# Three-layer attention and MLP kernel on one core: the first group gets a program of its own, one product for the gates, a token-major down product, and x normalised by ScalarE

## The reference

```
x  = x + proj(attention(q from ada_ln(x), k, v from ada_ln(ctx)))          # CROSS0
s  = silu(cond) @ W_mod + b_mod      -> shift_a scale_a gate_a shift_m scale_m gate_m
x  = x + gate_a * proj(self_attention(ln(x) * (1 + scale_a) + shift_a))    # SELF1
x  = x + proj(attention(q from ln(x), k, v from ln(ctx)))                  # CROSS1
h  = gelu((ln(x) * (1 + scale_m) + shift_m) @ W_mlp1 + b_mlp1)
x  = x + gate_m * (h @ W_mlp2 + b_mlp2)                                    # MLP
```

## Time and profile before

| | |
|---|---|
| median of 3 runs | 320.36 us (318.62 to 321.75) |
| the profiled execution's own time | 321.06 us |
| its span | 319.3 us |
| busy: PE, DVE, ACT, POOL | 273.6, 237.2, 199.4, 129.5 us |
| first scores of unit 0 start (PE L440) | 31.50 us |
| unit 0's attention is transposed (PE L493) | 57.41 us |
| unit 47's attention is transposed (PE L493) | 290.60 us |
| last DVE instruction ends | 316.5 us |

### The profile page before, as it was taken

How to read it: one execution, slowest core, us unless ns; L and a number is a source line. 1 busy time by engine, 2 the same in 40 slices (tenths; PEclk the granted TensorE clock), 3 DMA queues, 4 the chain that set the end, 5 groups by cost and what they waited for, 6 DMA issues and landing times.

```text
span 319.3 us, 9897 instructions
## 1 busy us (share of the span) xinstructions
PE 273.6 (86%) x3731; PEld 172.9 (54%) x3731; DVE 237.2 (74%) x503; ACT 199.4 (62%) x344; POOL 129.5 (41%) x257
## 2 busy tenths in 40 slices
PE   0555669799999899999999999999999899989983
PEld 0422345566656566566666666666666555544441
DVE  6854884977979879789798897988979796311422
ACT  2234236558686776677666666677676768799560
POOL 8553832723525235253472654636435131200100
PEclk9985756969999999999999999999999999999999
DMA  6953331321323414133141331312414100000112
GB/s 194 285 162 109 99 104 42 101 66 30 107 71 89 117 53 118 52 89 103 54 114 41 102 106 52 101 55 78 129 54 114 43 4 4 3 3 1 33 33 66
DMA packets 31902, 25.36 MB, mean 79 GB/s; under 512 B 4552, under 2 KB 31600, under 8 KB 31856
## 3 DMA queue, kind: packets, MB, share of 16 engines
q1 hardware_dynamic: 30240, 23.49, 26.3%
q10 hardware_dynamic: 1616, 1.25, 1.4%
HBM read 4.41 MB, written 1.05 MB: 17 GB/s over the span
## 4 chain that ended last, share of the span: by engine, by line
PE 55%; DVE 26%; issue 8%; ACT 8%; POOL 1%; ACTq 1%; DVEq 0%; POOLq 0%
DVE neg_max L838 13%; PE all_ps L477 11%; PE all_ps L415 9%; PE score_ps L440 5%; PE keyed_ps L463 5%; PE all_ps L508 4%; PE all_ps L517 4%; PE all_ps L405 4%; PE all_ps L500 3%; PE all_ps L488 3%; DVE x_stats L805 3%; ACT parts L636 3%; PE all_ps L398 2%; DVE r_sum L853 2%; DVE normed L819 2%
## 5 line engine op out<-in xcount | busy, mean ns | idle before, releaser
L838 DVE TENSOR_REDUCE neg_max<-score_ps 128x8 f32<-128x1024 f32 x96 | 116.9, 1218 | 9.3 <-PE score_ps L440 8.6
L656 ACT ACTIVATE probs<-keyed_ps 128x1024 f32<-128x1024 f32 x96 | 98.4, 1025 | 18.4 <-PE keyed_ps L463 18.2
L477 PE MATMUL all_ps<-probs,values 128*32 128x128 f32 x1536 | 62.1, 282 | 2.1 <-ACT probs L656 2.1
L477 PEld LDWEIGHTS all_ps<-probs,values 128*32 128x32 f32 x1536 | 37.0, 110 | 21.2 <-issue 9.5
L440 PE MATMUL score_ps<-stack_k,stack_q 62*128 62x128 bf16 x768 | 40.0, 227 | 9.6 <-DVE neg_max L838 9.6
L664 ACT ACTIVATE summed<-all_ps 128x256 f32<-128x256 f32 x48 | 18.4, 383 | 38.0 <-PE all_ps L477 38.0
L440 PEld LDWEIGHTS score_ps<-stack_k,stack_q 62*128 62x128 bf16 x768 | 22.7, 97 | 32.0 <-DVE neg_max L838 20.9
L463 PE MATMUL keyed_ps<-stack_q,stack_k 64*128 64x128 bf16 x768 | 38.6, 221 | 0.7 <-ACT probs L656 0.7
L989 POOL CAST max_parts<-neg_max 128x16 bf16<-128x16 f32 x48 | 10.1, 210 | 65.1 <-DVE neg_max L838 65.0
L621 ACT ACTIVATE normed_t<-all_ps,mod 128x128 f32<-128x128 f32 x48 | 18.0, 460 | 28.9 <-PE all_ps L405 18.8
L982 POOL TENSOR_TENSOR rstd<-var_eps,minus_half 128x4 f32<-128x4 f32 x24 | 25.4, 1059 | 18.0 <-DVE var_eps L807 18.0
(11 more groups left out here) (97 smaller groups left out, 395.6 us busy)
## 6 DMA issues: line engine op xcount, KB each, us to landing
stack_q<-parts SPq DMA_DIRECT2D x72, 128.0 KB, 2.4
stack_k<-parts SPq DMA_DIRECT2D x72, 128.0 KB, 2.4
stack_q<-max_rows SPq DMA_DIRECT2D x96, 4.0 KB
xs<-in_x_dram SPq DMA_DIRECT2D x4, 256.0 KB, 7.0
cs<-in_ctx_dram SPq DMA_DIRECT2D x4, 256.0 KB, 6.4
out_dram<-xs SPq DMA_DIRECT2D x4, 256.0 KB, 2.3
w<-in_L_xcond_W_mlp_dram SPq DMA_DIRECT2D x2, 256.0 KB, 4.2
wmod<-in_L_xcond_W_mod_dram ACTq DMA_DIRECT2D x1, 384.0 KB, 4.3
```

Source lines behind the costliest of these rows:

```text
L477: mm = pe.matmul(ps[QUAD * a:QUAD * (a + 1), c * T:(c + 1) * T], values[:, u // PER % STACKS, u % PER * PAIRS + CP * c + a, 2 * e:2 * e + ...
L656: act.activation(probs[:, n % 3, :], keyed_ps[:, :, :].rearrange("t e n -> t (e n)"), ACT.Exp, scale=float(D) ** -0.5).then_inc(probs_read ...
L838: dve.tensor_reduce(neg_max[:, u % 2, :, CP * c:CP * (c + 1)], score_ps[:, :, :].rearrange("t e (a k) -> t e a k", k=T), AX.X, ALU.max, ne ...
```

## The change

- **Head.** The first group is taken out of the tick loop: each engine has a straight program for `setup` and the front of group 0, and the loop starts at tick -6 rather than -10. `cond` is transposed before silu. DVE modulates the first context tile and splits the first k; ACT issues the first group's six k moves. The fills of the rings stand in other places. The late modulations move from tick 0 to tick 2.
- **Gates.** One product of 16 rows by 256 columns in tick 1; its rows go to DRAM and sixteen DMAs, one a tick, spread them over 128 partitions. `c_rep` is no longer filled, and the eight gate ticks are gone.
- **Normalising x.** POOL also computes minus the mean and the offset; ACT writes `normed` for x. The context stays on DVE.
- **Order.** `project_v` takes its bank before `project_qk(g, 0)`; ACT's second half of `modulate` for x comes behind the exponential; SP's moves are re-ordered.
- **MLP.** The down product has tokens as its rows, 8 steps of 2 sequences, 8 products of 128 columns each. The transposes back and ACT's bias step are gone; POOL adds gate times bias to x beforehand. Stores are halved in size.

```diff
+        gate_d = nc.dram_tensor("gate_d", [B, 2 * H], F32, kind="Internal").ap()
...
-        FIRST = -10
+        FIRST = -6
         LAST = 57
-        GATES_AT = (16, 19, 20, 23, 24, 27, 28, 31)
-        UP_AT = (43, 43, 44, 44, 45, 46, 46, 46, 47, 47, 48, 48, 52, 52, 52, 52)
-        DOWN_AT = (48, 48, 49, 49, 49, 49, 50, 50, 50, 50, 50, 50, 53, 53, 53, 53)
-        TURN_AT = (49, 50, 52, 55)
-        GELU_AT = (48, 49, 50)
+        UP_AT = (41, 43, 44, 45, 46, 46, 46, 48, 48, 48, 49, 49, 52, 53, 53, 53)
+        DOWN_AT = (49, 49, 50, 50, 51, 51, 53, 56)
+        GELU_AT = (48, 50, 51)
+        ADD_AT = (49, 50, 50, 51, 51, 51, 52, 53)
+        ACT_NORMS = (0,)
...
+            def put_gates():
+                sp.wait_ge(gate_rows_ready, 1)
+                sp.dma_start(gate_d, gate_rows[:, :, :].rearrange("b a h -> b (a h)")).then_inc(gate_put, 16)
+
+            def spread_gate(b):
+                if b == 0:
+                    sp.wait_ge(gate_put, 16)
+                sp.dma_start(gate[:, b, :, :].rearrange("t a h -> t (a h)"),
+                             gate_d[b:b + 1, :].broadcast_to([128, 2 * H])).then_inc(gate_landed, 16)
...
+            def gates():
                 w = wmod[:, :].rearrange("k (a n) -> k a n", n=H)[:, 2:6:3, :]
+                pe.matmul(take("gate")[0:B, 0:2 * H], c_col[:, :], w, start=True, stop=True).then_inc(gate_ps, 1)
...
+                pe.wait_ge(hidden_ready, MLP * (q + 1))
+                ps = take("down", 2 * q + c)
+                for j in range(2):
+                    for i in range(MLP):
+                        mm = pe.matmul(ps[:, j * H:(j + 1) * H], hidden_of(q, i)[:, (2 * c + j) * T:(2 * c + j + 1) * T],
+                                       w2[:, i, :], start=(i == 0), stop=(i == MLP - 1))
+                mm.then_inc(mlp_ps, 1)
 
             setup()
+            transpose_normed(0, 0)
+            transpose_normed(0, 1)
+            project_qk(0, 0)
+            project_qk(0, 1)
+            project_v(0)
...
+            def normalise_act(g, n):
...
+                for j in range(PER):
+                    ins = act.activation(normed[:, n, j, :], src[:, b0 + j, :], ACT.Identity,
+                                         bias=offset[:, n, j:j + 1], scale=rstd[:, n, j:j + 1])
+                ins.then_inc(normed_ready[n], 1)
...
+            modulate(0, 0, True)
+            modulate(0, 0, False)
+            first_part(0, 0)
+            first_part(0, 1)
+            act.wait_ge(hi_ready, 2)
+            act.wait_ge(stack_ones, 1)
+            for t in (0, 3, 5):
+                act.dma_start(stack_k[t:128:LANE, 0, :, :], parts[:, 0, 1, 0, :]).then_inc(k_landed[0], 16)
+            copy_values(0)
+            act.wait_ge(k0_split, 1)
+            for t in (1, 4):
+                act.dma_start(stack_k[t:128:LANE, 0, :, :], parts[:, 0, 1, 1, :]).then_inc(k_landed[0], 16)
+            act.wait_ge(k0_split, 2)
+            act.dma_start(stack_k[2:128:LANE, 0, :, :], parts[:, 0, 1, 2, :]).then_inc(k_landed[0], 16)
...
+            def add_mlp_bias(q):
...
+                pool.tensor_tensor(gate_b[:, :, :], gate[:, PER * q:PER * (q + 1), 1, :],
+                                   b_mlp[:, :].unsqueeze(1).broadcast_to([128, PER, H]), ALU.mult).then_inc(gate_b_ready, 1)
...
+                pool.wait_ge(normed_ready[0], GROUPS + q + 1)
+                pool.tensor_tensor(xs[:, PER * q:PER * (q + 1), :], xs[:, PER * q:PER * (q + 1), :],
+                                   gate_b[:, :, :], ALU.add).then_inc(x_biased, 1)
```

More of the change, by code:

```diff
@@ L45 @@
 RINGS = (("all", 4),)
-RING_KINDS = (("attn", "max", "turn", "proj", "out", "cond", "mod", "bias", "late", "norm", "q", "k", "v", "gate", "mlp", "up", "down"),)
+RING_KINDS = (("attn", "max", "turn", "proj", "out", "cond", "mod", "bias", "late", "norm", "q", "k", "v", "gate", "up", "down"),)
 R_Q, R_K, R_V = (0, 3, 6), (1, 4, 7), (2, 5, 8)
@@ L234, in at_tick @@
             uses += [("norm", g, 1)] * (g is not None)
+            g = attention(front(tick, -7))
+            uses += [("v", g)] * (g is not None)
             g = attention(front(tick, -8))
             uses += [("q", g)] * (g is not None)
-            g = attention(front(tick, -7))
-            uses += [("v", g)] * (g is not None)
-            uses += [("gate", i) for i in range(B // 2) if GATES_AT[i] == tick]
             uses += [("turn", tick - 1)] * unit(tick - 1)
@@ L556, in _ @@
                     keyed_scores(tick, 1)
+                g = attention(front(tick, -7))
+                if g is not None:
+                    project_v(g)
                 g = attention(front(tick, -8))
@@ L571, in _ @@
                     attend(tick, 0)
-                for n in range(MLP * B // PER):
+                if tick == 1:
+                    gates()
+                for n in range(B // 2):
                     if DOWN_AT[n] == tick:
-                        mlp_down(n // MLP, n % MLP)
-                if tick in TURN_AT:
-                    turn_mlp(TURN_AT.index(tick))
+                        mlp_down(n // 2, n % 2)
         @block.scalar
@@ L721, in _ @@
                     modulate(g, 0, False)
-                if unit(tick):
-                    exponentials(tick, 1)
-                g = front(tick, -8, 1)
+                for n in range(MLP * B // PER):
+                    if UP_AT[n] == tick:
+                        leave_hidden(n)
+                g = attention(front(tick, -7))
                 if g is not None:
-                    modulate(g, 1, False)
+                    copy_values(g)
                 g = attention(front(tick, -8))
@@ new lines, in modulate_context, with split_first_k @@
+            def modulate_context():
+                dve.wait_ge(normed_ps[1], 1)
+                dve.wait_ge(mod_ready, 2)
+                for j in range(PER):
+                    ins = dve.tensor_scalar(normed_t[:, 1, j, :], bank("norm", 0, 1)[:, j * T:(j + 1) * T],
+                                            mod[:, M_KV_SCALE, j:j + 1], mod[:, M_KV_SHIFT, j:j + 1], ALU.mult, ALU.add)
+                ins.then_inc(normed_t_ready[1], 1)
+            def split_first_k():
+                dve.wait_ge(rest_ready, 2)
+                dve.tensor_copy(parts[:, 0, 1, 1, :], rest[:, 1, :]).then_inc(k0_split, 1)
+                dve.wait_ge(k0_split, 1)
+                dve.tensor_tensor(parts[:, 0, 1, 2, :], rest[:, 1, :], parts[:, 0, 1, 1, :], ALU.subtract).then_inc(k0_split, 1)
```

345 lines of the change are left out of this document (186 added, 159 removed).

## The result

The changed kernel takes 305.26 us (median of 4 runs, 304.43 to 307.22) where the kernel before, run beside it, takes 320.97; the ratio is 0.955 with an interval of 0.951 to 0.959. The profiled execution took 304.43 us, with a span of 302.6. The forecast was 298.5, the range 290 to 307. So the size came out inside the range, at the value of the first rival (305), and 6.8 us above the forecast. One execution of a later kernel (joined, with the fillers) took 310.93 us at a granted clock of 0.85 for nearly its whole length, where the three others took 297.60 to 299.34, and is left out of its figures.

A forecast was written before the change was run, and what follows sets the result against it. PE was taken to set the loop's pace, with DVE close behind. Gates -7.7, loop -3.0, head -6, start-up -3 and tail -2.4 summed to -22.1 from 321.06, so 299.0; the forecast was 298.5 us, range 290 to 307.

The forecast's parts named there:

- the first rival: Loop gives nothing beyond the gates, ACT's load and later k moves taking the order's gain: about 305 us, chance 0.15.
- Gates, -7.7: In the loop's eight gate ticks, sixteen 256-column products go, all on PE's path: 7.7 us less.
- The loop's order, -3.0: In the loop, v-product and exponential waits go, DVE is relieved, ACT's normalising costs: -3.0 us, between -6 and +2.
- the +2.1: In the loop, ACT's normalising of x delays what PE needs by 0.2 us a group over eleven groups: +2.1 us.
- The gain of -1 from DVE's relief: In the loop, taking x's normalising off DVE relieves 1 us of PE's 4.2 us wait for row maxima.
- The head, -6: Before the first scores: they come at about 25.5 instead of 31.50 us; -6 us, between -3 and -8.
- the prediction's own sign of being wrong: In the head: the prediction is wrong if the first scores come after 29 us.
- The start-up, -3: At the loop's start, moved work and no c_rep fill give back half-clock time: -3 us, between 0 and -5.
- The tail, -2.4: At the MLP end, bias, transposes and waits shrink while down products grow dearer: -2.4 us, between +1 and -4.
- The second: Loop and start: all 8.3 us of waits go and the clock stays up, 3 us more: about 290, chance 0.10.
- the fourth: Head and tail move nothing that counts: half clock eats the earlier start, token-major products cost 0.29 each; 309, chance 0.06.

The follow-up runs named there:

- joined, with the fillers: Changed kernel plus MLP's x normalised by DVE, two POOL fills kept clear, ACT's group-1 normalising and a ring fill earlier, nine unread PE products: 297.64 us, ratio 0.932.
- the run with the gates alone: Kernel before with only the gates changed: one product at tick 1, rows spread through DRAM by 16 DMAs, no c_rep; 313.35 us, ratio 0.980.
- the run with the fills kept clear: Changed kernel with POOL's first two fills of values delayed until DVE normalised the first context and split the first k; 304.93 us, ratio 0.950.

## Why the prediction was right or wrong

The traced executions are 16.7 us apart, where -22.1 was forecast. Gates and order together gave the loop 6.5 of 10.7, the head 2.5 of 6 to the first scores, the start-up more than its 3, the tail 2.2 of 2.4. That the sum fell inside the range is in part luck: two of the five terms failed, a third gave more than forecast, and the tail's came out as the difference of two amounts that were not in it. Two sums are also off as written: 0.2 us over eleven groups is 2.2 and not 2.1, and the start-up's parts add up to -2.7, rounded to -3.

**Gates, -7.7: size near, working wrong.** Their run gave 6.9. But "all of it is on the path" failed: of 7.7 us of products the loop gave back 5.2, since half of the gate ticks also had a wait that overlapped them. What made up for it stood in another term: the `c_rep` fill that went with the gates gave 2.6 us at the start-up. So I had that money in two places.

**The loop's order, -3.0: failed, it gave 1.3.** Three steps. First, "The v product now takes its bank ahead of q, so 2.3 us of waits should go": they stayed, 2.3 us. Four banks back from v stands k, both before and after; q is taken in another tick, so the exchange of the two changes nothing there. Counting the ring back by its length in the order of uses would have shown it. Second, the waits for exponentials did go as predicted; the modulation in one piece brings back 2.7 us. Third, ACT's four instructions take 1.65 us, not 1.4, and they cost the loop half of the +2.1: 0.13 us in one tick of four, 1.1 together, through `summed`, as the run with x on DVE shows. The gain of -1 from DVE's relief did not come as a wait gone: between units 4 and 36 PE waits 3.9 us for the maxima, 4.0 in the run with the gates alone. But in the new order DVE could not have kept the work for nothing, it would cost 1.2 us.

**The head, -6: too large, by wrong placing.** The first scores moved 2.5 us, to 29.03, just past the prediction's own sign of being wrong. The stall was real, with 3.20 us for four instructions and 2.41 for a cast, but the step "Last come the context tiles of group 1, on DVE, beside POOL's fills" named the wrong tiles. The first fill stands right behind the inverse root of the context of group 0 and meets its normalising, ahead of every product; the second meets the cast of k. Here the rule of the Trainium skill (SBUF — State Buffer, Who interferes with whom) bears on it: the trace agrees that a fill holds DVE up, 0.45 us against 2.41 for the same cast, and what I missed was only when each fill runs. The same thing spoils a reading: the 1.61 us of the earlier trace rows at 4.08 us, put down to the shape of 16 partitions, end at 5.69, and a fill of POOL ran from 3.79 to 5.61. With 128 partitions by 16 and no fill beside it the step took 0.17 us; no run has the old shape without the fill. The second miss is ACT's queue: I had the k moves done by 18.4, they ended at 22.5, and at 21.1 with both fills moved.

**The start-up, -3: mechanism right, size too small.** It gave 3.6 from unit 0 to unit 4, and the stretch before it 1.8 more than the first scores account for (4.3 against 2.5). The 3.6 are mostly the clock, as the step said: "Up to 3 us of the time at half clock can come back; I take -2". In the kernel before it fell to 0.50 at 63.0, near the end of the idle 2.01 us of the earlier trace rows, and stayed there until 69.8. With the same fill but PE kept busy it stayed at 1.00. For the 1.8 the clock is likely but not isolated from the modulations that moved out: the clock rose at 52.7 us before and at 47.1 after, and the run with the MLP's x on DVE, whose program up to unit 0 is that of the changed kernel, took 25.3 us from the first scores to unit 0 with a rise at 49.5, where the changed kernel took 24.05.

**The tail, -2.4: the size right, 2.2, in part by luck.** The parts at the end are right: down products of 0.24 us each (0.245 taken), nothing between the last product and DVE's last pair. But with x on DVE the same new tail takes 75.0, 4.8 less than before, twice the forecast; ACT's normalising of the MLP's x, which the term has at nothing, takes 2.6 of it back. And the gain lies ahead of the last attention: from unit 36 to unit 47 the kernel takes 48.19 us instead of 51.14, from there to the end 29.4 instead of 28.7. What the term did not see either is that the new order of ACT needs the new tail: the old one in its place costs 7 us, not 2.4, of which about 1.7 are the clock's fall in that execution.

**The rivals.** The first gave 305 and the time is 305, but its mechanism is absent: no scores wait for k. The second was wrong about waits (of its 8.3 us only the 1.8 for exponentials went) and right about the clock. That the half clock would eat the earlier start (the fourth) is half true: in the run with the fills kept clear 0.9 of 1.4 us were gone by unit 0, and its clock rose 0.5 us later. The fourth's other half failed: the small products cost 0.24, not 0.29.

## What to carry to other kernels

Where several edits share a tick, price each alone and then ask what each covers: here the gates cost 5.2 us of the loop in one order and 8.7 in another, and a product that waits 0.26 us for a bank was the cover of a wait three times as long. For a ring of banks, count back by its length in the order of uses before a wait is written off. And where an engine idles for 2 us at the start, look at the granted clock of what follows before adding up durations: they may be halved or doubled by a fill elsewhere.

## What the runs showed of the hardware

- The granted clock of PE was 0.50 from 19.7 to 47.1 us in the changed kernel, but for 3.4 us at 1.00 from 33.4 on, with PE busy for 15.7 of the 25 us after 22. With nine unread products in its waits, 17.0 of 25 busy, one execution had 1.00 throughout. Two such products in one idle stretch of 2 us kept the clock up for the 7 us behind it.
- The moment at which the clock comes up in the head differed between two traces whose head has the same program: at 47.1 us in one, at 49.5 in the other, and unit 0 with it by 1.0 us (53.08 and 54.09).
- A POOL memset of 128x2048 float32 (1.8 us) held up DVE instructions that read SBUF in float32: a cast of 128x512 took 2.41 us instead of 0.45, four tensor_scalar of 128x128 3.20 instead of 1.37, one of 128x32 1.43 instead of 0.18. Others went on beside such a fill: a memset by DVE of 128x2048 took its plain 1.76 us (the kernel before, 10.62 us), an addition that reads PSUM its plain 0.23 us (the run with the fills kept clear, 9.05 us).
- ACT takes 0.41 us for each 128x128 operation in a row from SBUF with scale and bias by partition (1.65 for four), against 0.375 from PSUM (1.50 for four).
- A DMA issued by ACT holds its queue for 0.60 to 0.76 us, and arithmetic behind it waits.
